# A hybrid model on one core: softplus product moved into PSUM and shared with GpSimd, state-space decays ahead of a copy, layer norms rearranged

## What is computed

```python
x = edge_attention_block(x)               # two layer norms with gain and shift, one small MLP
x = x + rope_attention(group_norm(x))
t = t + attention(ln_t(t))
t = t + moe_ffn(ln_t(t))                  # 8 experts, top 2 by softmax
t = t + mamba(ln_t(t))                    # 6 state-space layers, then an rmsnorm
t = t + moe_ffn2(ln_t(t)); layer_norm with gamma, beta
```

```python
u, z = split(rmsnorm(res) @ in_w)
uc   = silu(conv4(u) + cb)
dt_r, B, C = split(uc @ xp_w)             # 16 states
dt   = softplus(dt_r @ dt_w + dt_b)
h_t  = exp(dt_t * A) * h_{t-1} + dt_t * u_t * B_t      # 128 channels x 16 states
y    = (h * C summed over states + D * uc) * silu(z)
res += y @ out_w
```

## Time and profile before

| what | value |
|---|---|
| time, median of 3 runs | 472.26 us (467.3 to 472.62) |
| profiled execution, its own time | 465.5 us |
| span of its profile | 463.7 us |
| mean granted clock of TensorE | 0.876 |
| busy: PE / DVE / ACT / POOL | 342.8 / 333.4 / 250.8 / 204.1 us |
| first `dbu` drive to last gate (L925 at 204.52, L891 at 431.45) | 226.9 us |

### The profile page before, as it was taken

One profiled execution on the slowest core, in us unless ns is written; L12 is line 12 of the kernel. 1 busy time (PEld: TensorE's weight loads), 2 busy tenths in 40 slices (PEclk: granted clock), 3 DMA queues, 4 the chain that ended last, 5 costly groups with the idle time before them and its releaser, 6 DMA issues.

```text
span 463.7 us, 5642 instructions
## 1 busy us (share of the span) xinstructions
PE 342.8 (74%) x1700; PEld 229.7 (50%) x1700; DVE 333.4 (72%) x583; ACT 250.8 (54%) x673; POOL 204.1 (44%) x208
## 2 busy tenths in 40 slices
PE   4964479866985796358887888878887888786482
PEld 2563345544554533125564655646555566554251
DVE  2994576637883514167989889898898898989563
ACT  2301048823881552467667686676866767764060
POOL 0750080000000000258669597596876958855000
PEclk9985568978998698559989999899999999998767
DMA  7700000000000000051441514406234142250000
GB/s 254 316 1 0 1 0 2 1 0 1 2 0 1 0 1 1 0 184 27 157 172 48 185 37 185 182 1 220 53 129 183 39 182 87 98 183 1 0 0 12
DMA packets 10400, 34.16 MB, mean 74 GB/s; under 512 B 2200, under 2 KB 2568, under 8 KB 10248
## 3 DMA queue, kind: packets, MB, share of 16 engines
q1 hardware_dynamic: 10376, 33.88, 20.6%
HBM read 33.49 MB, written 0.38 MB: 73 GB/s over the span
## 4 chain that ended last, share of the span: by engine, by line
DVE 37%; PE 33%; issue 14%; ACT 11%; POOL 2%; DMA 1%; DVEq 1%; SPq 0%; ACTq 0%; POOLq 0%
DVE big L937 13%; PE PS L557 4%; DVE dt L905 4%; PE PS L351 3%; DVE big L944 3%; DVE big L925 3%; PE PS L268 2%; PE PS L516 2%; PE PS L369 2%; ACT PS L1157 2%; PE PS L431 2%; PE PS L536 2%; PE PS L379 2%; PE PS L479 2%; DVE big L778 2%
## 5 line engine op out<-in xcount | busy, mean ns | idle before, releaser
L937 DVE TENSOR_TENSOR_SCAN big<-PS,big 128x1024 f32<-128x1024 f32 x48 | 109.5, 2285 | 16.9 <-ACT PS L1157 16.2
L1334 POOL TENSOR_TENSOR big<-dtu,big 128x1024 f32<-128x1024 f32 x36 | 84.2, 2355 | 46.5 <-DVE dtu L912 46.5
L1157 ACT ACTIVATE PS<-dt,amat 128x255 f32<-128x255 f32 x192 | 80.4, 462 | 39.0 <-DVE dt L909 35.9
L557 PE MATMUL PS<-big,cst 128*128 128x256 f32 x384 | 94.9, 399 | 1.5 <-DVE big L944 1.5
L557 PEld LDWEIGHTS PS<-big,cst 128*128 128x128 f32 x384 | 73.4, 198 | 18.4 <-DVE big L944 5.1
L1275 POOL TENSOR_TENSOR hbias<-wmt,half_t 128x1 f32<-128x1 f32 x6 | 1.1, 190 | 115.6 <-PE PS L494 115.6
L944 DVE TENSOR_TENSOR big<-big,PS 128x1024 f32<-128x1024 f32 x36 | 43.8, 1217 | 1.6
L1028 ACT ACTIVATE big<-PS 128x512 f32<-128x512 f32 x43 | 25.5, 597 | 34.2 <-PE PS L351 10.2
L1065 ACT ACTIVATE big<-PS,big 128x256 f32<-128x256 f32 x64 | 29.6, 472 | 15.3 <-DVE big L770 15.3
L536 PE MATMUL PS<-stack,pick_b 96*128 96x256 bf16 x144 | 22.7, 282 | 18.7 <-DVE big L944 10.2
L1342 POOL TENSOR_TENSOR big<-big 128x1024 f32<-128x1024 f32 x12 | 28.3, 2356 | 0.4 <-DVE big L937 0.4
(11 more groups left out here) (260 smaller groups left out, 663.3 us busy)
## 6 DMA issues: line engine op xcount, KB each, us to landing
big<-spill SPq DMA_DIRECT2D x48, 512.0 KB, 5.6
wmt<-in_wm SPq DMA_DIRECT2D x6, 418.0 KB, 3.2
w3t<-in_w SPq DMA_DIRECT2D x1, 1588.0 KB, 13.5
w2t<-in_w SPq DMA_DIRECT2D x1, 896.0 KB, 10.2
cst<-in_const SPq DMA_DIRECT2D x1, 848.0 KB, 8.0
w5t<-in_w SPq DMA_DIRECT2D x1, 812.0 KB, 15.0
w0t<-in_w SPq DMA_DIRECT2D x1, 416.5 KB, 3.6
w1t<-in_w SPq DMA_DIRECT2D x1, 385.0 KB, 8.5
```

The lines of the kernel that those rows point to most:

```text
L557: last = pe.matmul(yps, ident, hc[:, g, s], start=False, stop=(g == NSG - 1 and s == SG - 1))
L937: v.tensor_tensor_scan(flat(hst[g][:]), flat(da[g % 2]), flat(dbu[:, g]), 0.0, ALU.mult, ALU.add).then_inc(sem("m_h"), 1)
L1157: one = act.activation(da[g % 2][:, n, 1:N], dt[b][:, 1:N], ACT.Exp, scale=amat[k][:, col:col + 1])
L1334: pool.tensor_tensor(dbu[:, g], dtu[b][:].unsqueeze(1).to_broadcast([P, SG, N]), bsp[b][:, SG * (g - 1):SG * g], ALU.mult).then_inc(sem("m ...
```

## The change

1. `sp_u` (exp(-|x|)) lies in PSUM (bank 7) in place of SBUF, and VectorE multiplies into it. VectorE multiplies two quadratics into it; GpSimd adds the constants to the other two and multiplies them (`prep_quartic`), and VectorE multiplies by that product. VectorE has 5 instructions in `prep_dt` where it had 6. ScalarE does the relu ahead of the exponential.
2. The four decays of group 3 are issued together, ahead of `xds`.
3. `stack` has other parts: ScalarE copies the middle part (`prep_middle`), GpSimd makes one remainder (`prep_rest`) and the low part (`prep_low`, behind the quartic), in place of four GpSimd instructions.
4. A layer's weights are prepared on GpSimd and ScalarE at the end of an even unit, one unit earlier than before.
5. Norms: the mean is subtracted from all 256 columns in one instruction, and where there is a gain it is applied, before the wait for the rate; the rate is applied in one instruction. The norm of a norm takes its rate from the first variance in closed form, without statistics of its own. The first unit's rmsnorm likewise: GpSimd makes its rate, VectorE `hs2`. In the group norm two small copies and one small product are gone.
6. The closing rmsnorm of the state-space stage handles batch 0 ahead of the last gate. The last norm's `beta` is added to X ahead; the last addition and the output DMA go by halves.

```diff
-        sp_u, sp_m = two("sp_u", [P, N]), two("sp_m", [P, N])
+        sp_u, sp_m = PS[:, 7, 0:N], two("sp_m", [P, N])
...
+            def ln_scale(n, j, src, dst):
+                v.wait_ge(sem("ln_rstd"), n)
+                v.tensor_tensor(dst, src, rstd[:, j].unsqueeze(2).to_broadcast([P, NG, D]), ALU.mult)\
+                    .then_inc(sem("ln_norm"), 1)
...
+            def ln(n, j, src, dst, gain=None, shift=None):
+                ln_mean(j, src)
+                mean = mv[:, j, :, 0:1].to_broadcast([P, NG, D])
...
+                    chain(v.tensor_tensor(dst, src, mean, ALU.subtract))
                     v.wait_ge(sem("ld_rows"), 16)
...
+                    chain(v.tensor_tensor(dst, dst, row(gain), ALU.mult))
+                ln_scale(n, j, dst, dst)
...
-            ln(3, Xg, Yg)
-            v.wait_ge(sem("ln_norm"), 4 * NG)
-            ln(4, Yg, Zg)
+            ln_mean(3, Xg)
+            chain(v.tensor_tensor(Zg, Xg, mv[:, 3, :, 0:1].to_broadcast([P, NG, D]), ALU.subtract))
+            ln_scale(4, 3, Zg, Yg)
+            v.wait_ge(sem("ln_norm"), 4)
+            ln_scale(5, 4, Zg, Zg)
...
+            ln_mean(5, Xg)
+            chain(v.tensor_tensor(Yg, Xg, mv[:, 5, :, 0:1].to_broadcast([P, NG, D]), ALU.subtract))
+            v.wait_ge(sem("u0_rate"), 2)
+            first = rstd[:, 8].rearrange("p (a b) -> p a b", b=B)[:, :, 0]
+            v.tensor_tensor(hs2[0][:].rearrange("p a (c e) -> p a c e", c=2),
...
             def prep_dt(u, b):
 
-                for q in range(4):
+                for q in range(2, 4):
                     cq = quadratics()[q][2]
-                    v.wait_ge(sem("m_q"), u * 5 + q + 1)
-                    if q > 0:
-                        v.wait_ge(sem("m_poly"), u * 4 + q)
-                    src = sp_u[b][:] if q == 0 else dt[b][:]
-                    v.scalar_tensor_tensor(dt[b][:], sp_q[b][:, q], cq, src, ALU.add, ALU.mult)\
+                    v.wait_ge(sem("m_q"), u * 4 + 4)
+                    if q > 2:
+                        v.wait_ge(sem("m_poly"), u * 3 + 1)
+                    v.scalar_tensor_tensor(sp_u, sp_q[b][:, q], cq, sp_u, ALU.add, ALU.mult)\
                         .then_inc(sem("m_poly"), 1)
-                v.wait_ge(sem("m_poly"), u * 4 + 4)
-                v.wait_ge(sem("m_q"), u * 5 + 5)
-                v.tensor_tensor(dt[b][:], dt[b][:], sp_m[b][:], ALU.add).then_inc(sem("m_dt"), 1)
+                v.wait_ge(sem("m_quartic"), u * 3 + 3)
+                v.wait_ge(sem("m_poly"), u * 3 + 2)
+                v.tensor_tensor(sp_u, sp_u, sp_q[b][:, 0], ALU.mult).then_inc(sem("m_poly"), 1)
+                v.wait_ge(sem("m_poly"), u * 3 + 3)
+                v.wait_ge(sem("m_relu"), u + 1)
+                v.tensor_tensor(dt[b][:], sp_u, sp_m[b][:], ALU.add).then_inc(sem("m_dt"), 1)
...
+            v.wait_ge(sem("m_res"), UNITS - 1)
+            final_square(0)
+            final_gain(0)
             gate(UNITS - 1, 1, 1)
             residual(UNITS - 1, 1)
...
-            ln(7, Yg, Zg, "gamma", "beta")
-            v.wait_ge(sem("ln_out"), 6)
-            v.tensor_tensor(Zg, Zg, Xg, ALU.add).then_inc(sem("result"), 1)
+            ln(8, 7, Yg, Zg, "gamma")
+            v.wait_ge(sem("ln_norm"), 8)
+            for a in range(HALF):
+                v.tensor_tensor(half_tm(Z, a), half_tm(Z, a), half_tm(X, a), ALU.add).then_inc(sem("result"), 1)
...
+            def prep_middle(u, b):
+
+                act.wait_ge(sem("m_rest"), u + 1)
+                act.activation(stack[b][0:64], rest[0:64], ACT.Copy).then_inc(sem("m_mid"), 1)
...
-                decay(u, k, b, 3, range(2))
+                decay(u, k, b, 3)
                 if not last:
                     prep_xd(u + 1, nk, nb)
-                decay(u, k, b, 3, range(2, SG))
-                if not last:
                     prep_softplus(u + 1, nk, nb)
-
...
+                    prep_middle(u + 1, nb)
+                if s in (0, 2, 4):
+                    layer_loaded(act, i, s + 2)
+                    prep_weights(1 - k)
...
+            def prep_quartic(u, b):
+
+                for q in range(2):
+                    pool.wait_ge(sem("m_q"), u * 4 + q + 1)
+                    if q == 0:
+                        pool.wait_ge(sem("m_rest"), u + 1)
+                    pool.tensor_tensor(sp_q[b][:, q], sp_q[b][:, q], quad_t[:, 4 + q:5 + q].to_broadcast([P, N]),
+                                       ALU.add).then_inc(sem("m_quartic"), 1)
+                pool.wait_ge(sem("m_quartic"), u * 3 + 2)
+                pool.tensor_tensor(sp_q[b][:, 0], sp_q[b][:, 0], sp_q[b][:, 1], ALU.mult).then_inc(sem("m_quartic"), 1)
...
                 if not last:
-                    if b == 0:
-                        prep_rates(i, s + 1, k)
                     prep_gz(u, b)
-                    prep_stack(u, b)
-
-
-            pool.wait_ge(sem("x_out"), 1)
+                    prep_rest(u, b)
+                    prep_quartic(u, b)
+                    prep_low(u, b)
+                if s in (0, 2, 4):
+                    pool.wait_ge(sem("m_stack"), u + 1)
+                    prep_weights(i, s + 2, 1 - k)
+                    prep_rates(i, s + 2, 1 - k)
```

More of the change, by code:

```diff
@@ L316, in _ @@
             last.then_inc(sem("f0_y"), 1)
-            to_T2(X, PS[:, 3, 0:N], "ln_out", 4, "turned")
+            to_T2(X, PS[:, 3, 0:N], "ln_out", 2, "turned")
             pe.wait_ge(sem("g_stats"), 1)
-            pe.matmul(PS[:, 6, 0:2], CONST.of(cst, "pairs"), small[:, 0:2], start=True, stop=True).then_inc(
+            pe.matmul(PS[:, 6, 0:2], CONST.of(cst, "pairs"), mv[:, 8, 0, 0:2], start=True, stop=True).then_inc(
                 sem("g_pair"), 1)
@@ L647, in _, with ln_mean @@
         def _(v):
-            def ln(j, src, dst, gain=None, shift=None):
+            seen = [0]
+            def ln_mean(j, src):
                 for g in range(NG):
@@ L652, in ln @@
                 for g in range(NG):
-                    v.wait_ge(sem("ln_stats"), j * NG + g + 1)
+                    v.wait_ge(sem("ln_stats"), seen[0] + g + 1)
                     v.bn_aggr(mv[:, j, g], stats[:, j, g]).then_inc(sem("ln_aggr"), 1)
[L655 to L659, removed]
+                seen[0] += NG
+                v.wait_ge(sem("ln_aggr"), seen[0])
+            def ln_scale(n, j, src, dst):
[5 more added lines that the diff above has]
+                mean = mv[:, j, :, 0:1].to_broadcast([P, NG, D])
+                if gain is None:
+                    chain(v.tensor_tensor(dst, src, mean, ALU.subtract))
+                else:
+                    chain(v.tensor_tensor(dst, src, mean, ALU.subtract))
                     v.wait_ge(sem("ld_rows"), 16)
-                    v.wait_ge(sem("ln_norm"), (j + 1) * NG)
-                    v.tensor_tensor(dst, dst, row(gain), ALU.mult).then_inc(sem("ln_out"), 1)
-                    v.wait_ge(sem("ln_out"), {0: 1, 1: 3, 7: 5}[j])
+                    chain(v.tensor_tensor(dst, dst, row(gain), ALU.mult))
+                ln_scale(n, j, dst, dst)
+                if shift is not None:
+                    v.wait_ge(sem("ln_norm"), n)
                     v.tensor_tensor(dst, dst, row(shift), ALU.add).then_inc(sem("ln_out"), 1)
@@ L735, in _ @@
             chain(v.tensor_copy(small[:, 2:4], PS[:, 6, 0:2]))
[L736 to L737 removed]
+            v.scalar_tensor_tensor(small[:, 5:6], small[:, 2:3], small[:, 2:3], small[:, 3:4],
+                                   ALU.mult, ALU.subtract).then_inc(sem("g_var"), 1)
             v.wait_ge(sem("g_rstd"), 1)
@@ L952, in _, with final_square, final_gain @@
                 v_step(0, s, last=(s == 11))
+            scaled = hs2[0][:].rearrange("p a (b e) -> p a b e", b=B)
+            normf = ROWS.of(rowt, "normf").unsqueeze(1).to_broadcast([P, HALF, D])
+            power = small[:, 0:4].rearrange("p (a b) -> p a b", b=B)
+            def final_square(b):
+                chain(v.tensor_tensor(Z[:, :, b], Y[:, :, b], Y[:, :, b], ALU.mult))
+                v.tensor_reduce(power[:, :, b], Z[:, :, b], AX.X, ALU.add).then_inc(sem("n_sum"), 1)
+            def final_gain(b):
+                chain(v.tensor_tensor(scaled[:, :, b], Y[:, :, b], normf, ALU.mult))
+            v.wait_ge(sem("m_res"), UNITS - 1)
+            final_square(0)
+            final_gain(0)
             gate(UNITS - 1, 1, 1)
@@ L1015, in _ @@
             v.memset(y_ones, 1.0).then_inc(sem("y_b2w"), 1)
+            chain(v.tensor_tensor(Xg, Xg, row("beta"), ALU.add))
             v.wait_ge(sem("y_y"), 1)
@@ L1197, in _ @@
             prep_softplus(0, 0, 0)
+            prep_middle(0, 0)
             a_step(0, 0, first=True)
```

149 lines of the change are left out of this document (75 added, 74 removed).

## The result

Before: 471.05 us median of four executions (467.3 to 472.62). After: **454.94** (454.78 to 455.09), a ratio of 0.9669 with a 95% interval of 0.9607 to 0.9731. The forecast was 454.

A forecast was written before the change was run, and what follows sets the result against it. VectorE was taken as the bound, with TensorE half a microsecond behind and deciding the gain. State-space units 7.8 us plus norms 9.8 make 17.6 off the median 472.26: 454.7, rounded to 454 us, range 446 to 463.

The forecast's parts named there:

- The wait for the decays goes, and TensorE is the bound: State-space units: VectorE's 1.34 us wait goes; TensorE's 24 unbroken sums (5.35) and `spread_b` set the drive at 357.30.
- The first rival: State-space units: TensorE is not the bound, the whole 1.34 us comes back in 11 passages, 448 us; chance 0.06.
- 0.87 a unit: State-space units: the next first drive comes at 357.30 against 358.17, a gain of 0.87 us.
- Nine units of eleven gain: State-space stage: two of 11 passages have a slower TensorE clock and gain nothing, so 9 x 0.87 = 7.8 us.
- Where TensorE's clock falls, nothing is gained: Units with the lower clock: 24 sums took 6.76 us with the drive straight behind them, so gain 0.
- The third rival: State-space units: slower clock in six of 11 units, stage gives 4.4 us, time 458 us; chance 0.17.
- The second rival: State-space units: the softplus comes 0.9 us later and becomes the new wait, only norms pay, 462.5 us; chance 0.17.
- The fourth rival: State-space units: GpSimd holds VectorE in all five instructions, 0.67 us each, 11.8 us slower, 484 us; chance 0.04.
- The norms: Norms, entry into the first unit, closing rmsnorm and end: together 9.8 us saved, all on the chain.
- The norm of a norm: First scale at 0.60, transposes 1.65 us after the statistics in place of 4.15: 2.5 us saved.
- Into the first unit: Statistics to transposes in 1.55 us in place of 4.4: 2.8 saved, less 0.5 for the first softplus, 2.3.
- The base: Whole kernel: gains taken from the runs' median, 472.26 us, giving 454.7, not from the profiled 465.5, giving 447.9.

The follow-up runs named there:

- experiment 2: The kernel after with group 3's four decays split around the copy of `xds` again: 457.28 us, ratio 0.976.
- experiment 3: The kernel before with one edit, group 3's four decays issued together ahead of `xds`: 463.98 us, ratio 0.986.
- the first profile: The kernel before, unchanged, profiled in its fastest execution, 465.5 us; the prediction was made from it.
- the second: The kernel before, unchanged, profiled a second time: 471.33 us.
- experiment 5: The kernel after with one idle TensorE product of 256 columns in each of two stops per unit, ahead of the products for `uc` and `xds`: 448.68 us, ratio 0.956.
- experiment 6: The kernel after with the two idle products per unit and all four quadratics on VectorE: 447.42 us, ratio 0.955.
- experiment 10: The kernel before with one idle TensorE product in each of the same two stops per unit: 467.95 us, ratio 0.995.
- experiment 8: The kernel after without the 33 idle products of L548: 473.01 us, ratio 1.002.
- experiment 1: The kernel before with the changed norms alone, state-space layers untouched except the product entering the first unit: 456.33 us, ratio 0.975.
- experiment 7: The kernel after with `sp_u` in SBUF in place of PSUM: 458.93 us, ratio 0.969.
- experiment 4: The kernel after with all four quadratics multiplied by VectorE, none by GpSimd, product still in PSUM: 455.85 us, ratio 0.973.

## Why the prediction came out right, step by step

**The wait for the decays goes, and TensorE is the bound.** Right, to 0.01 for TensorE and the drive; the softplus was ready 0.24 to 0.36 earlier than forecast. On the scale of the earlier trace rows (times of after plus 25.22), the squares ended at 353.84 (forecast 354.2), the quartic product at 354.80 (355.15), `dtu` started at 355.86 (356.1), `spread_b` ended at 357.25 (357.26), and the drive came at 357.29 (357.30). The 24 sums took 5.34 of a forecast 5.35. The drive comes 0.04 behind `spread_b` and the scan waits for nothing, as both had been named; experiments 2 and 3 show that it is the decays that did it. The first rival, the whole 1.34 back, falls with them.

**0.87 a unit.** Measured 1.04: undisturbed passages went from 18.89 to 17.85. The 0.17 on top lies ahead of `uc`: from the first drive to `uc` took 9.43 and takes 9.23. It is not the weights that were moved away from there: behind the first passage of before, the five with them took 9.32 to 9.54 to `uc` and the five without 9.27 to 9.51, and experiment 3 leaves them in their place and has 9.27 to 9.34 in eight of ten. GpSimd's rows show most of it, first of before (L925 at 339.29), then of after (L953 at 314.27):

```profile
339.25 2.36 POOL L1334 TENSOR_TENSOR big<-dtu,big 128x1024 f32<-128x1024 f32 x1 [4.50 <-DVE dtu L912]
...
342.62 0.61 POOL L1299 TENSOR_TENSOR hs<-Y,rms 128x256 f32<-128x256 f32 x1
```

```profile
313.56 2.35 POOL L1393 TENSOR_TENSOR big<-dtu,big 128x1024 f32<-128x1024 f32 x1 [1.02 <-DVE dtu L940]
...
317.45 0.62 POOL L1349 TENSOR_TENSOR hs<-Y,rms 128x256 f32<-128x256 f32 x1
```

With `dtu` ready well ahead of the drive, GpSimd's own first drive starts 0.71 ahead of VectorE's where it started beside it. The norm's scale `hs` behind it then comes 3.18 behind the drive for 3.33, and with it the transposes, `ht`, the decays of group 2, their scan and `uc`. Where a weight at the end of the unit before holds GpSimd's drive back to 0.03 to 0.12 ahead, `uc` comes at 9.36 to 9.39 instead. No run tried this by itself. I had taken the way to `uc` as unchanged.

**Nine units of eleven gain.** This is the term of the sum that failed most: 9 x 0.87 = 7.8 measured 6.1 to 6.9. Two passages behind the first were disturbed in the profile that I had; four are in after. And a fall now costs 1.70 on 17.85, the whole 1.69 by which the sums are stretched, where it cost 0.9 on 18.9: VectorE was the bound there and hid the rest. "Where TensorE's clock falls, nothing is gained" holds about: 19.78 before, 19.55 after, 0.23. So six passages gave their 1.04 and four some 0.2 or, where before had no fall, less than nothing (19.55 for 18.9), and the stage came to 6.1 on the first profile and 6.9 on the second, for 7.8. The third rival had the mechanism, at six units; I didn't see that the changed kernel would itself have more falls. Filling two of TensorE's stops takes them all away (experiments 5, 6 and 10), and emptying another brings more (8). But before has the same two stops and only one or two falls, experiment 1 two, experiments 2 and 3 four and three: why the state-space edits raise the number stays open.

**The softplus.** The second rival needed `dtu` at 356.62 or later; it came at 355.86. GpSimd's hold on `dtu` is there, 1.01 for 0.43, which is 0.58 in this unit (bounded at 0.73). It acts like a start at 356.44, still under 356.62, so it costs nothing, but only 0.2 of slack is left in such a unit. What the Trainium skill's page "SBUF — State Buffer", section "Who interferes with whom", has as a lock between the two engines, the runs bear out: with the product in SBUF three kinds of instructions and GpSimd's own are stretched, with it in PSUM only `dtu` is. The fourth rival, slower by five such holds, has its mechanism in experiment 7 and not its price: with `sp_u` in SBUF `dtu` starts 0.79 later in a unit without a weight, which just uses up the slack, and in a unit with one an estimated 0.8 would be left over, hidden there by the falls. VectorE reading or writing PSUM costs nothing (424 to 432 ns, where I had allowed 0.05 each).

**The norms.** Forecast 9.8, measured 8.6 between fixed rows, so this term was too large by 1.2. Their timeline in after, first the norm of a norm, then the entry into the first unit, the first unit's drive, and the end:

```profile
147.84 0.36 DVE L656 BATCH_NORM_AGGREGATE mv<-stats 128x2 f32<-128x6 f32 x4
...
148.88 0.43 DVE L663 TENSOR_TENSOR Y<-Z,rstd 128x256 f32<-128x256 f32 x1 [0.21 <-ACT rstd L1080]
...
149.84 0.67 PE L260 MATMUL PS<-cst,Z 128*128 128x128 f32 x2
...
184.76 0.42 POOL L1426 TENSOR_SCALAR lnv<-mv 128x4 f32<-128x4 f32 x1 [87.50 <-DVE mv L656]
185.27 1.04 POOL L1428 TENSOR_TENSOR rstd<-lnv,power_t 128x4 f32<-128x4 f32 x1
186.41 0.43 DVE L897 TENSOR_TENSOR hs<-Y,rstd 128x256 f32<-128x256 f32 x1 [1.28 <-POOL rstd L1428]
186.89 0.69 PE L502 MATMUL PS<-cst,hs 128*128 128x128 f32 x2 [3.60 <-DVE hs L897]
...
201.46 1.03 PE L527 MATMUL PS<-stack,pick_b 96*128 96x256 bf16 x4 [4.58 <-POOL stack L1370]
202.53 1.22 DVE L953 TENSOR_TENSOR big<-dtu,PS 128x1024 f32<-128x1024 f32 x1 [0.45 <-PE PS L527]
...
450.12 1.17 SPq L250 DMA_DIRECT2D out<-Z  x2
```

- The norm of a norm: 1.64 from the end of the statistics (148.20) to the second transposes where it was 4.15 from 148.00; the gain is 2.51 there and 2.41 at the products behind them, forecast 2.5; the sum has 2.41.
- Two with gain 1.48 (1.4), two without 0.95 (1.1), group norm 0.32 (0.35), closing norm 0.65 (0.7), the end 1.33 (1.4).
- **Into the first unit: 1.44 where I had 2.3.** The power on 128x4 took 1.04, and I had priced it at 0.73 by an instruction 64 times as large; with its predecessor's 0.42, GpSimd needs 1.55 ahead of VectorE's product. And the first softplus lost 0.73 for my 0.5: `spread_b` waits 4.58 for GpSimd's low part of `stack`, which now stands behind the quartic, and the drive waits for `spread_b`.

**The base.** I took the gain from the median and not from the profiled execution, 454.7 and not 447.9. The result bears that out, but partly by luck. The terms measured 14.7 to 15.5 together (6.1 or 6.9, and 8.6) where I had 17.6. Two things made up for it: before's median was 471.05 with one more execution, 1.2 lower, and the median fell by 16.1, 0.6 to 1.4 more than the terms. That lies outside the units, in stretches whose clock differs from profile to profile, and I had no term for it. Kernels with the same instructions up to the first drive as after (experiments 2, 5 and 8) reached it at 199.1 to 200.6, and 4 and 6, without GpSimd's part in the first softplus, at 198.7 and 200.2; after itself at 202.53, with a mean clock of 0.78 where 2 and 5 had 0.82. All four executions of after lie within 0.3 us, so this is no chance of one execution. What sets where the clock falls ahead of the units wasn't found; it is worth 2 to 3.4 us here, up to half as much as the whole state-space change, and stays open.

One slip in the chances: the parts named for "faster by over 2%" add up to 0.85 and not 0.83. The stated 0.8 holds about.

## What to carry to other kernels

Once the chain of another engine is some half a microsecond behind the one that bounds, work out both and take the later: 0.87 was TensorE's number, 1.4 VectorE's, and the drive came within 0.01 of TensorE's. When a change makes TensorE the bound, look for falls of its clock too, since each is then paid in full; two idle products a unit, in stops of half a microsecond, gave 6 us where the change to the layers gave 6 to 7. And judge a part of a change by its own stretch: the clock of a stretch whose instructions were the same moved its end by 2 to 3.4 us.

## What the runs showed that I had not expected

- With no stop of TensorE over 0.8 in a unit behind the first, its clock still fell to 1.2 GHz in four of ten units; with one idle product in each of the two stops of 0.71 and 0.47 it fell in none. Without the 33 idle products of L548 every passage was lengthened, and the mean clock of 100 us was 0.78.
- The clock of the stretch ahead of the units differs between kernels whose instructions there are the same: 0.78 in after, 0.82 in the fifth kernel.
- A `tensor_tensor` power of GpSimd on 128x4 took 1.04, longer than its 128x256 product (0.73).
- VectorE reading and writing PSUM (429 ns) is as fast as an undisturbed product in SBUF (425 ns).
